# Self attention: the probabilities turned by VectorE in squares of 32 and by a trip through DRAM, instead of by TensorE

## The reference, cut to what matters

```
n  = layernorm(x)                                  # (4, 1024, 512)
qk = einsum('bsd,btd->bst', n, k)                  # k: (1, 2048, 512)
p  = softmax(qk * scale[:, None, :], axis=-1)      # scale: the four normalised rows n[b, ::256], one after the other
x  = x + einsum('bst,btv->bsv', p, v)              # v: (1, 2048, 512)
```

## Time and profile before

| | us |
|---|---|
| three runs | 3888.32, 3894.85, 3895.75 |
| median | 3894.85 |
| the profiled execution: first to last instruction | 3891.2 |
| self attention in it (to the last `add`) | 813 |

### The profile page before, as it was taken

One profiled execution on the slowest core, in us unless ns is written; L12 is line 12 of the kernel. 1 busy time (PEld: TensorE's weight loads), 2 busy tenths in 40 slices (PEclk: granted clock), 3 DMA queues, 4 the chain that ended last, 5 costly groups with the idle time before them and its releaser, 6 DMA issues. The chain is left out here.

```text
span 3891.2 us, 63669 instructions
## 1 busy us (share of the span) xinstructions
PE 3788.4 (97%) x19001; PEld 2532.2 (65%) x19161; DVE 2395.0 (62%) x6222; ACT 1432.7 (37%) x1793; POOL 1534.5 (39%) x860
## 2 busy tenths in 40 slices
PE   8999999999999899999999999999999999999998
PEld 7888888888877444544444444544444777777776
DVE  6544444444458688888888788878887533433135
ACT  3111222233224455455545555445555221222332
POOL 1000000000013667766677666766665222312234
PEclk9999999999999999999999999999999999999999
DMA  4001000145555322222112222222111433328579
GB/s 157 32 32 32 32 32 32 44 172 178 191 179 186 94 57 55 57 57 46 35 38 57 58 57 58 54 57 55 33 36 49 151 126 132 114 92 278 185 263 332
DMA packets 223177, 381.89 MB, mean 98 GB/s; under 512 B 17544, under 2 KB 102056, under 8 KB 222892
## 3 DMA queue, kind: packets, MB, share of 16 engines
q1 hardware_dynamic: 192876, 301.34, 26.7%
q0 software_dynamic: 14752, 49.29, 3.5%
q10 hardware_dynamic: 15264, 27.79, 1.9%
HBM read 229.71 MB, written 148.66 MB: 97 GB/s over the span
## 5 line engine op out<-in xcount | busy, mean ns | idle before, releaser
L1103 DVE CUSTOM_DVE_ANT_0 xf_unread<-xa_mx_ps,mask_q 128x402 bf16<-128x402 f32 x1984 | 1036.0, 573 | 290.3 <-PE xa_mx_ps L1096 156.7
L1726 ACT ACTIVATE probs<-xa_scores 128x1024 f32<-128x1024 f32 (+1 forms) x416 | 417.5, 1024 | 417.0 <-PE xa_scores L1600 371.6
L1726 ACT ACTIVATE xa_probs<-xa_scores 128x1024 f32<-128x1024 f32 (+1 forms) x416 | 417.3, 1024 | 397.8 <-PE xa_scores L1600 355.1
L1561 POOL TENSOR_TENSOR xa_sums<-xa_sums,xa_probs 128x1024 f32<-128x1024 f32 x220 | 519.7, 2383 | 18.1 <-POOL xa_sums L1561 15.7
L1561 POOL TENSOR_TENSOR xa_sums<-xa_sums,probs 128x1024 f32<-128x1024 f32 x220 | 519.3, 2381 | 18.9 <-POOL xa_sums L1561 15.3
L1600 PE MATMUL xa_scores<-mask_t,ident_b 128*128 128x512 bf16 (+1 forms) x1505 | 499.7, 387 | 5.3 <-issue 0.2
L1096 PE MATMUL xa_mx_ps<-xa_kp,queries 96*128 96x402 f32 x1024 | 364.2, 418 | 0.8
L1096 PE MATMUL xa_mx_ps<-xf_kp,queries 96*128 96x402 f32 x960 | 341.5, 418 | 0.4
L1594 PE MATMUL xa_scores<-queries,xf_kp 97*128 97x512 f32 (+1 forms) x832 | 284.2, 423 | 16.3 <-ACTq L1748 8.2
L1096 PEld LDWEIGHTS xa_mx_ps<-xa_kp,queries 96*128 96x128 f32 x1024 | 181.7, 189 | 172.2 <-DVE xf_maxima L1103 111.6
L1594 PE MATMUL xa_scores<-queries,xa_kp 97*128 97x512 f32 (+1 forms) x832 | 284.7, 423 | 1.8 <-ACT probs L1726 1.8
(11 more groups left out here) (415 smaller groups left out, 7388.0 us busy)
## 6 DMA issues: line engine op xcount, KB each, us to landing
bridge_rows<-sorted_in SPq DMA_DIRECT2D x78, 256.0 KB
sorted_out<-ex_made ACTq DMA_DIRECT2D x78, 256.0 KB
queries<-qT_high SPq DMA_DIRECT2D x30, 512.0 KB
xf_kp<-kT_high SPq DMA_DIRECT2D x16, 800.5 KB, 12.4
xa_kp<-kT_high SPq DMA_DIRECT2D x16, 800.5 KB
rows<-in_ctx SPq DMA_DIRECT2D x16, 768.0 KB, 5.1
values<-cxl_v SPq DMA_DIRECT2D x48, 256.0 KB
kT_high<-cxl_kT_high SPq DMA_DIRECT2D x12, 768.0 KB, 4.0
```

What stands on the lines that cost most here:

```text
L1103: return dve.tensor_tensor_reduce(out=unread[slot % 2][:, :], in0=scores[:, 0:MKEYS], in1=mask_q[:, half * QB + qt, MFIRST[kb]:MFIRST[kb] ...
L1561: pool.tensor_tensor(sums[pr][:, :, :], left[pr][:, :, :], right[pr][:, :, :], ALU.add).then_inc(pool_added, 1)
L1726: act.activation(prob[ring][pr][0:keys, :, :], scores[pr][0:keys, :, :], ACT.Exp, scale=SCALE).then_inc(exped, 1)
```

## The change

The PE transposes of the probabilities go. VectorE turns `prob` in squares of 32 by 32 in one instruction and writes them into `scaled`; SP stores that tile to a DRAM tensor `turned_p` (1 MB), waits for it to land, and loads it back in four strips, each into 32 partitions of `prob`. There the probabilities stand with the keys on the partitions. ScalarE takes the high part from SBUF and GpSimd, no longer VectorE, the low part. Freed PSUM tiles are only renamed. The core of the diff:

```diff
+SQUARE = 32
+QB = P // SQUARE
+MOVED = 16 * QB
+        prob_by_key = prob.rearrange("p j (c a k) -> p a (j c) k", a=QB, k=SQUARE)
+        squares = scaled.rearrange("p a (c q) -> p a c q", q=SQUARE)
+        raw_pT = prob.rearrange("p i (c q) -> p c i q", q=SQUARE)
+        def wait_moved(eng, t):
+            eng.wait_ge(p_in, MOVED * (t + 2))
+        AHEAD = GROUPS_W - FULL
@@ sync
+                def move(t):
+                    sp.wait_ge(p_turned, t + 1)
+                    sp.dma_start(turned_p, scaled).then_inc(p_out, 16)
+                    sp.wait_ge(p_out, 16 * (t + 1))
+                    for a in range(QB):
+                        sp.dma_start(prob[a * SQUARE:(a + 1) * SQUARE, :, :],
+                                     turned_p[:, a, :].rearrange("(i k) n -> k i n", k=SQUARE)).then_inc(p_in, 16)
                 load_add(0)
+                move(0)
                 for b in range(1, B):
                     load_scale(b)
+                move(1)
                 store(0)
                 with sp.Fori(0, tiles - 3) as t:
                     load_norm(t + 3)
                     load_add(t + 1)
+                    move(t + 2)
                     store(t + 1)
@@ gpsimd
+                def low_p(t):
+                    for j in range(NB):
+                        mine = slice(j * KB, (j + 1) * KB)
+                        pool.wait_ge(pT_high, NB * t + j + 1)
+                        pool.tensor_tensor(pT[1][:, mine, :]..., raw_pT[:, mine, :, :],
+                                           words(pT[0][:, mine, :])..., ALU.subtract).then_inc(pT_low, 1)
+                with pool.Fori(0, tiles - 3 - B) as t:
+                    step(t + B + 3)
+                    low_p(t + B + 1)
@@ tensor
-                def turn_p(t, j): ...
                 def tile(t, ahead):
-                    if ahead >= 1:
-                        for j in range(NB - 1):
-                            score(t + 1, j)
-                    turn_p(t, 0)
-                    turn_p(t, 1)
-                    if ahead >= 1:
-                        score(t + 1, NB - 1)
+                    for j in range(NB) if ahead >= 1 else ():
+                        score(t + 1, j)
                     if ahead >= 2:
                         turn(t + 2)
+                    for n in range(AHEAD) if ahead == 0 else ():
+                        turn_last(n)
                     for j in range(NB):
                         weigh(t, j)
-                        if j + 2 < NB:
-                            turn_p(t, j + 2)
@@ scalar
                 def exp(t):
-                    act.wait_ge(p_turned, NB * t + 1 + NB)
+                    act.wait_ge(pT_low, NB * (t + 1))
                 def high_p(t, j):
                     if j == 0:
                         act.wait_ge(weighed, t + 2)
+                        wait_moved(act, t)
+                    act.activation(pT[0][:, mine, :]..., raw_pT[:, mine, :, :], ACT.Copy).then_inc(pT_high, 1)
                 def tile(t, ahead):
+                    for j in range(NB):
+                        high_p(t, j)
                     if ahead >= 2:
                         high_n(t + 2)
                     if ahead >= 1:
                         exp(t + 1)
@@ vector
                 def scale_block(t, j):
                     if j == 0:
-                        dve.wait_ge(exped, t + 2)
+                        wait_moved(dve, t - 1)
-                def low_p(t, j): ...
+                def turn_p(t):
+                    dve.wait_ge(exped, t + 3)
+                    dve.transpose(squares[:, :, :, :], prob_by_key[:, :, :, :]).then_inc(p_turned, 1)
                 def tile(t, ahead):
                     invert(t); normalize(t + 2); scale_block(t + 1, 0 to 2) with next_scales(t, 0 to 2)
-                    low_p(t, 0)
-                    low_p(t, 1)
                     scale_block(t + 1, NB - 1); row_max(t + 1); low_n(t + 2); next_scales(t, NB - 1)
+                    if ahead >= 1:
+                        turn_p(t + 1)
                     add(t)
```

More of the change, by code:

```diff
@@ L130, in self_attention @@
         nT_ps = ps("nT_ps", [P, DC, P])
-        pT_ps = [ps(f"pT_ps{i}", [P, KB, P]) for i in range(2)]
+        k_ps = [ps(f"k_ps{i}", [P, KB, P])[:, :, :] for i in range(2)]
         o_ps = ps("o_ps", [P, D])
-        k_ps = [pT_ps[0][:, :, :], pT_ps[1][:, :, :], o_ps[:, :].rearrange("p (c n) -> p c n", n=P)]
+        k_ps.append(o_ps[:, :].rearrange("p (c n) -> p c n", n=P))
         raw_in = [sem(f"raw_in{i}") for i in range(ARRIVALS)]
@@ L231, in _ @@
                     load_add(t)
+                    if t == tiles - 2:
+                        move(t + 1)
                     if t == tiles - 1:
-                        sp.wait_ge(exped, tiles + 2)
+                        wait_moved(sp, tiles - 1)
                         sp.dma_start(opening.rows[:, 0, 0:FULL, :],
                                      context[0][0:FULL * P, :].rearrange("(r p) n -> p r n", p=P)).then_inc(rows_in, 16)
-                        sp.wait_ge(p_turned, NB * tiles + NB + 1)
+                        sp.wait_ge(pT_low, NB * tiles + NB)
                         sp.dma_start(opening.rows[:, 1, 0:FULL, :],
@@ L266, in _ @@
                                        ALU.subtract).then_inc(v_low_pool, 1)
[L267 to L272, removed]
+                pool.sem_inc(pT_low, NB)
+                for t in range(B + 1):
+                    step(t + 2)
+                    low_p(t)
+                    if 0 < t < B:
+                        scale_step(t)
+                with pool.Fori(0, tiles - 3 - B) as t:
+                    step(t + B + 3)
+                    low_p(t + B + 1)
+                low_p(tiles - 2)
+                low_p(tiles - 1)
             @block.tensor
@@ L298, in score @@
                     last.then_inc(scored, 1)
[L300 to L306, removed]
                 def weigh(t, j):
@@ L333, in tile @@
                 def tile(t, ahead):
-                    if ahead >= 1:
-                        for j in range(NB - 1):
-                            score(t + 1, j)
-                    turn_p(t, 0)
-                    turn_p(t, 1)
-                    if ahead >= 1:
-                        score(t + 1, NB - 1)
+                    for j in range(NB) if ahead >= 1 else ():
+                        score(t + 1, j)
                     if ahead >= 2:
                         turn(t + 2)
+                    for n in range(AHEAD) if ahead == 0 else ():
+                        turn_last(n)
                     for j in range(NB):
                         weigh(t, j)
-                        if j + 2 < NB:
-                            turn_p(t, j + 2)
-                        for n in range(FULL) if ahead == 0 else ():
-                            turn_last(FULL * j + n)
-                    for n in range(FULL * NB, LAST_GROUPS) if ahead == 0 else ():
+                        if ahead == 0 and AHEAD + j < GROUPS_W:
+                            turn_last(AHEAD + j)
+                    for n in range(GROUPS_W, LAST_GROUPS) if ahead == 0 else ():
                         turn_last(n)
                 pe.sem_inc(turned, 2)
-                pe.sem_inc(p_turned, NB + 1)
                 pe.sem_inc(weighed, 2)
@@ L384, in high_p @@
                         act.wait_ge(weighed, t + 2)
-                    act.wait_ge(p_turned, NB * t + j + 2 + NB)
-                    act.activation(pT[0][:, j * KB:(j + 1) * KB, :], pT_ps[j % 2][:, :, :], ACT.Copy).then_inc(pT_high, 1)
+                        wait_moved(act, t)
+                    mine = slice(j * KB, (j + 1) * KB)
+                    act.activation(pT[0][:, mine, :].rearrange("p c (i q) -> p c i q", q=SQUARE), raw_pT[:, mine, :, :],
+                                   ACT.Copy).then_inc(pT_high, 1)
                 def high_last(n):
@@ L392, in tile @@
                 def tile(t, ahead):
-                    high_p(t, 0)
-                    high_p(t, 1)
+                    for n in range(NB) if ahead == 0 else ():
+                        high_last(n)
+                    for j in range(NB):
+                        high_p(t, j)
+                        if ahead == 0:
+                            high_last(NB + j)
+                    for n in range(2 * NB, LAST_GROUPS) if ahead == 0 else ():
+                        high_last(n)
                     if ahead >= 2:
                         high_n(t + 2)
[L397 to L402, removed]
                     if ahead >= 1:
@@ L537, in tile @@
                     next_scales(t, NB - 1)
[L538 to L542, removed]
+                    if ahead >= 1:
+                        turn_p(t + 1)
+                    for n in range(AHEAD) if ahead == 0 else ():
                         low_last(n)
                     add(t)
-                    for n in range(NB * FULL - FULL, LAST_GROUPS) if ahead == 0 else ():
+                    for n in range(AHEAD, LAST_GROUPS) if ahead == 0 else ():
```

(2 more changed lines are left out.)

16 lines of the change are left out of this document (8 added, 8 removed).

## The result

Timed beside each other on one chip, the changed kernel takes 3926.98 us (median of 4 runs, 3925.4 to 3927.48) and the kernel before 3895.3 (4 runs, 3888.32 to 3898.31): ratio 1.0088 [1.0074, 1.0102]. Forecast were 3923 and a chance of 71% for slower. In the profiled execution the span is 3925.7, 34.5 more than before.

What follows compares the result with a forecast made beforehand. The bound was to move from PE (22.6 us a tile) to a closed loop of 24.7 through VectorE, GpSimd, ScalarE, SP and DMA; with both ends, the stage ends 28.0 later: 3894.85 + 28 = 3923 us, range 3870 to 3985.

Steps and rivals of the forecast that it cites:

- step 1: SP's queue: x_norm's load, issued behind the strips and the store, lands 1.3 us after a tile's last strip.
- Rival A: Strips land at the full 400 GB/s, PE stays the bound at 22.6 us a tile: 3852 us, chance 17%.
- M: Landing of a tile's last strip, from which the loop is counted to the next; M(0), tile 0's, forecast at 57.45.
- Step 2: VectorE: statistics to first scale block 2.31 us, then the blocks and row max; peak ready at M + 8.4.
- Step 3: GpSimd beside VectorE: four low-part subtractions at 1.28 us each, from M + 3.1 to M + 8.3, level with VectorE's branch.
- Step 4: ScalarE: the exponential with its accumulator read, 2.09 us, ending at M + 10.7.
- Step 5: VectorE: the 2048-column turn, taken as 2.3 us (1.9 to 4.6), ending at M + 13.0.
- Rival B: Slower still: the turn or GpSimd's subtractions cost more, 3979 or 3997 us, half of either 3950 to 3960; chance 21%.
- Step 6: DMA: the 1 MB store from 128 partitions lands in 4.3 us, with hops ending at M + 17.4.
- Step 7: DMA: four strips into 32 partitions each, 5.1 us of data at 205 GB/s plus 2.05 fixed, 7.2; ends M + 24.7.
- rival C: No difference: the loop is shorter by 0.6 to 1.1 us, giving 3888 to 3903 us; chance 12%.
- rival D: PE's new idle time, some 2 us a tile, lowers its clock; left out of the sum, no chance given.

Runs made afterwards that it cites:

- norm_first: Changed kernel with x_norm's load issued on SP ahead of the round trip's move and store: 3852.88 us beside 3894.95 for the kernel before, ratio 0.9892.
- full_rate: Changed kernel with the four 32-partition strips replaced by four 256 KB loads over 128 partitions, keys not reordered: 3902.38 us, ratio 1.0027 to the kernel before.
- two_queues: Changed kernel with strips 0 and 1 issued by SP and strips 2 and 3 from ScalarE's queue: ratio 1.0027 to the kernel before.
- warm_end: Changed kernel with 52 dummy transposes in PE's last long idle time: 3909.59 us in one execution beside 3878.73 for the kernel before, ratio 1.008.

## Why the prediction was right, and where it was not

**The bound moved from PE to the loop over x_norm's load: right,** and shown by norm_first, which undoes nothing but step 1's order and has PE busy throughout at 22.6. Rival A (PE stays the bound) was true of the kernel one load away.

**The loop of 24.7: right as a sum (24.66 in the tile shown, 24.8 in the mean), by errors that cancel.** Step 1: M + 1.3, as forecast. Step 2: too small. The forecast took 2.31 from the statistics to the first scale block; it is 3.24 (614.36 to 617.60), since the normalisation, 0.55 in itself, stands 1.47 beside GpSimd's first subtraction. I had priced the subtraction on GpSimd and not what it does to DVE next to it. The Trainium skill has this (SBUF — State Buffer, "Who interferes with whom"): a `tensor_scalar` in a mode that uses both VectorE ports shares one pair with GpSimd, and whoever comes first holds it for a whole instruction. The trace agrees as far as it goes: the normalisation that began 0.07 behind GpSimd's first subtraction took 1.47, and the scale blocks beside the same subtractions, with one operand in PSUM, kept their 0.6; in which mode the normalisation ran no row shows. Step 3: GpSimd from M + 3.1 to M + 8.25, forecast 8.3. So the branches were not level: DVE's ended 1.1 later, and it released 30 of 32 exponentials. The same late normalisation is what PE waits for: its idle time stands before `turn(t+2)`, released by DVE, and not before `weigh`, released by GpSimd, as I had said it would show. Step 4: right (2.10). Step 5: the turn took 2.31, forecast 2.3 from the row max of as many columns. Rival B fell away with both its prices, 4.6 for the turn and 1.77 for a subtraction (1.29 each). The estimate that stood beside it (5.0, sixteen times the 311 ns of the Trainium skill, VectorE: DVE Perf Modes, "The three transpose paths") does not hold for one long turn; the measurement decides. Step 6: 3.86 with the hop where 4.4 stood; 4.3 was another store's landing. Step 7: 6.96 in this tile, 7.18 in the median, where 7.2 stood.

**Step 7 had the right size for a half wrong reason.** I took 5.1 of data at 205 GB/s over a fixed 2.05, and rival A's 4.6 from 400 GB/s. The data in the changed kernel did take about 5.0; but full_rate shows a median of 6.35 at full width, with about 4.0 of data and not 2.6. The narrow landing is 0.8 of the 7.2, not 2.5; the rest is that a load of a megabyte from DRAM takes 5.9 even as one transfer. So the price of rival A (3852) was wrong: full width did not bring the full rate, and gave a ratio of 1.0027. The sentence beside it, that the loop must be 0.9 shorter for a tie, is nearly borne out: full_rate and two_queues, 0.65 and 0.8 shorter in their period, end at 1.003. That is also rival C's case (a loop shorter by 0.6 to 1.1), a little above its 3888 to 3903.

**The stage as a whole: 10.0 too small, most of it at its ends.** M(0) 56.1 instead of 57.5 and tile 1 21.6 instead of 22.1, -1.8. Tiles 2 to 5, where scale rows are normalised, 113.8 (77.72 to 191.50) instead of 4 x 24.7 + 9.5 = 108.3, +5.5: these normalisations too took 0.9 and 1.5 instead of 0.53, 1.4 a tile in three tiles, by the same cause as in step 2 as far as the rows show (the third of a tile, begun when GpSimd was done, took 0.53); 1.3 of the 5.5 I can't place. 25 tiles at 24.81, +2.8, and the last tile 21.3, -0.8. Then 17.5 from landing to `add` instead of 13.1, +4.4: 2.4 for rival D, the clock, left out of the sum because "PE has 2 us to spare anyway", true inside and false behind the last landing, where nothing covers it; and 2.0 (warm_end's 15.05 less 13.1) for four groups of transposes at 0.45, one just ahead of the last weighing and three inside it, not in idle time as I had them. Inside the stage D was harmless: in the changed kernel, columns as at the top,

```profile
616.00:618.00 2.00, 0.27 (x2) 0.27 (x3) 1.80 (x2) 0.00 (x0) 2.00 (x3) 1.00 0.00 0
618.00:620.00 2.00, 2.00 (x9) 1.68 (x8) 2.00 (x4) 0.60 (x1) 2.00 (x2) 0.62 0.00 0
620.00:622.00 2.00, 2.00 (x6) 1.54 (x6) 1.97 (x2) 0.00 (x0) 1.30 (x2) 0.52 0.00 0
622.00:624.00 2.00, 2.00 (x11) 1.61 (x10) 0.99 (x2) 1.57 (x1) 0.00 (x0) 1.00 0.00 0
```

PE idles 2.0 us (1.73 in the first of these windows, 0.26 in the one before), runs 4 at nearly half speed, and the loop's slack takes it up. The stage's 38 became 34.5 in the span because the untouched rest was shorter in that execution, and the median of the runs lies 1.3 above the span where the sum had 3.65. So of the stage's error of 10.0 only 4 is left in the time (3923 for 3927); the other 6, 3.5 and 2.4, is luck.

## What to carry to other kernels

When work moves from a full engine to a chain of waits, count the chain from one member back to the same member and look in each issuing queue for a load that stands behind a wait of that chain: moving it can decide the sign (here from +0.9% to -1.1%). When work goes to GpSimd, price also what VectorE does beside it. A slack that covers a cost in every tile covers nothing behind the last one.

## What the runs showed of the hardware beyond that

- Over 128 partitions, a store of 1 MB to DRAM landed in 3.8 us, a load of the same megabyte in 5.9 as one transfer and in 6.35 (median) as four. Four stores of 256 KB from 32 partitions took 6.2 together, four loads into 32 partitions 7.2 (median; 6.9 to 8.3), and 6.3 when two queues issued them.
- A 128x512 f32 normalisation on VectorE, SBUF to SBUF, took 0.55 us alone and 1.47 beside a GpSimd subtraction that had begun 0.07 earlier.
- A turn in squares of 32 of 128x2048 in 4-byte numbers took 2.31 us on VectorE, the pace of its row max.
- PE's granted clock read 0.62 and 0.52 in the two stretches of 2 us after an idle time of 2.0 us, and 0.50 over 6 us after one of 5.7; the matmuls came 0.23 apart again 4.4 and 5.4 us after PE had gone back to work. With 52 dummy transposes in the place of the 5.7 us it read 1.00.
